# Joined exponentials, a transposed fold and a moved 1/sqrt in a two-layer Mamba, tree, attention and expert kernel

## The reference, cut to what matters

```python
# attention: 16 heads, 4 key/value heads, head width 64, causal, over each sequence
scores = einsum(q, k) / 8, masked above the diagonal
probs = softmax(scores)
out = (probs @ v) @ Wo
# experts: 64 experts, 8 for each token
scores = softmax(x @ gate_w.T)
topk_w, topk_ids = top_k(scores, 8);  topk_w /= topk_w.sum()
h = silu(x_e @ w_gate) * (x_e @ w_up);  out_e = h @ w_down
y = sum over the 8 of topk_w * out_e
# after each block
x = layernorm(x + block(x))
```

## Time and profile before

| | |
|---|---|
| time, median of 3 runs | 5111.49 us (5107.31 to 5113.56) |
| the profiled execution's own time | 5056.72 us |
| its span, first to last instruction | 5054.9 us |
| mean granted TensorE clock | 0.948 of full speed |
| attention, 1884 to 3712 us | 1828 us: TensorE busy 1767.73, VectorE 1575.48, ScalarE 1505.22, GpSimd 352.55 |
| route, 3712 to 4110 us | 398 us: TensorE 245.36, VectorE 182.49, ScalarE 116.57, GpSimd 277.73 |
| combine, 4892 to 5055 us | 163 us: VectorE 154.56, GpSimd 23.89, DMA engines 84% busy |

### The profile page before, as it was taken

The page is one execution under the profiler, slowest core; times in us unless marked ns, Lnnn a source line. Parts: engine busy times, 40 slices in busy tenths (PEclk is TensorE's granted clock), DMA queues, the critical chain, the costliest instruction groups (busy, mean ns, idle before and its releaser), DMA issues. The chain is left out here.

```text
span 5054.9 us, 84397 instructions
## 1 busy us (share of the span) xinstructions
PE 4342.6 (86%) x20410; PEld 3064.2 (61%) x20411; DVE 3700.1 (73%) x7521; ACT 2830.2 (56%) x6544; POOL 1747.8 (35%) x1517
## 2 busy tenths in 40 slices
PE   6887787769999879999999999999976649999960
PEld 2333333336666447888888888888865637777740
DVE  6999999966666678888888888888854433333349
ACT  6777777522222118888888888888843314444420
POOL 5777777620000011122121212122137743333321
PEclk8999999999999989999999999999987869999985
DMA  1000000021111461211121112212135445555558
GB/s 42 13 13 13 13 13 9 9 69 36 36 36 35 151 188 26 52 31 49 27 58 26 50 26 59 51 26 51 34 116 169 164 127 157 156 150 155 156 174 276
DMA packets 329081, 384.68 MB, mean 76 GB/s; under 512 B 124209, under 2 KB 263337, under 8 KB 323003
## 3 DMA queue, kind: packets, MB, share of 16 engines
q1 hardware_dynamic: 255931, 265.05, 17.8%
q0 software_dynamic: 26112, 73.44, 4.1%
q10 hardware_dynamic: 46944, 45.16, 3.3%
HBM read 230.26 MB, written 153.24 MB: 76 GB/s over the span
## 5 line engine op out<-in xcount | busy, mean ns | idle before, releaser
L1539 DVE TENSOR_TENSOR probsT<-ps_t,probsT 128x512 fp32r<-128x512 f32 (+3 forms) x1280 | 779.6, 609 | 137.8 <-ACT probsT L1479 116.2
L1479 ACT ACTIVATE probsT<-ps_t 128x512 fp32r<-128x512 f32 (+3 forms) x1280 | 686.6, 536 | 255.8 <-PE ps_t L1327 231.2
L1471 ACT ACTIVATE probs<-ps_s,negm 128x512 f32<-128x512 f32 (+3 forms) x1297 | 812.4, 627 | 28.1 <-DVE negm L1532 27.1
L1339 PE MATMUL ps_o<-probsT,vbuf 128*128 128x512 f32 (+3 forms) x2560 | 815.8, 402 | 6.8 <-ACT folding L1485 6.2
L1314 PE MATMUL ps_s<-kbuf,qbuf 128*128 (+1 forms) x2602 | 768.7, 380 | 59.2 <-ACT probs L1471 31.5
L1519 DVE TENSOR_REDUCE pmax<-ps_s 128x1 f32<-128x512 f32 (+3 forms) x1301 | 777.6, 600 | 48.6 <-PE ps_s L1314 24.3
L1327 PE MATMUL ps_t<-idn,probs 128*128 128x128 f32 x4352 | 694.8, 275 | 13.8 <-DVE probsT L1539 13.8
L445 POOL TENSOR_TENSOR dBx<-u,b_all 128x1024 f32<-128x1024 f32 x256 | 616.2, 2409 | 237.0 <-DVE h L531 226.3
L1327 PEld LDWEIGHTS ps_t<-idn,probs 128*128 128x128 f32 x4352 | 517.4, 142 | 135.2 <-DVE probsT L1539 41.0
L1314 PEld LDWEIGHTS ps_s<-kbuf,qbuf 128*128 128x128 f32 x2602 | 445.5, 189 | 179.0 <-issue 65.4
L1422 POOL CAST qbuf<-qstage 128x512 fp32r<-128x512 f32 x132 | 81.4, 616 | 1272.1 <-DMA qstage<-q_scr 748.1
(11 more groups left out here) (249 smaller groups left out, 7243.5 us busy)
## 6 DMA issues: line engine op xcount, KB each, us to landing
xr<-xs ACTq DMA_DIRECT2D x294, 136.0 KB
parts<-y SPq DMA_DIRECT2D x36, 1024.0 KB, 5.2
qstage<-q_scr SPq DMA_DIRECT2D x528, 64.0 KB
w_gu<-W_guT SPq DMA_DIRECT2D x64, 384.0 KB, 3.5
q_scr<-rot SPq DMA_DIRECT2D x64, 256.0 KB, 2.9
attn<-ostage SPq DMA_DIRECT2D x128, 128.0 KB, 2.0
at<-attn SPq DMA_DIRECT2D x32, 512.0 KB, 4.1
w_d<-W_downT SPq DMA_DIRECT2D x64, 192.0 KB, 3.7
```

The costliest lines, as they stand in the source:

```text
L1339: last = nc.tensor.matmul(ps_o[:, lo:], vbuf[:, kb, :, :], probsT[:, g % SLOTS, part, lo:], start=kb == 0 and part == 0, stop=kb == BAND * ...
L1471: nc.scalar.activation(probs[:, k, at:at + n, :], ps_s[:, u % RING, 0:n * P], ACT.Exp, bias=negm[:, tile, :], accum_out=sums[:, s, j, c:c ...
L1479: nc.scalar.activation(probsT[:, g % SLOTS, 0, lo:], ps_t[:, t % 2, lo:], ACT.Copy).then_inc(high_t.sem, 1)
L1539: nc.vector.tensor_tensor(probsT[:, g % SLOTS, 1, lo:], ps_t[:, t % 2, lo:], probsT[:, g % SLOTS, 0, lo:].bitcast(F32), ALU.subtract).then ...
```

## The change

Four parts.

1. **Joined exponentials.** A chunk that is not its tile's last and does not lie in the last bank of the ring is exponentiated together with the next one, in one ScalarE instruction over two PSUM banks (up to 1024 columns), at the first one's turn; the second one's turn has no `exps`. The semaphore rises by 2 at its end. `MERGE` pairs the chunks (0,1), (2,3), (5,6), (8,9), (10,11), (12,13) of unit 0 and (0,1), (3,4), (6,7), (10,11), (12,13), (16,17), (18,19) of unit 1: 13 pairs in a head. Since the exponentials run 16 chunks ahead, unit 0's chunks are done in unit 1's turns and the other way round.
2. **Fold by four transposes.** The fold is 4 transposes of 128x128 instead of 4 fp32 matmuls by `idn_2`. The two halves are no longer added by it: a new ScalarE copy `spill` takes the whole bank to `halves`, and GpSimd's `finish` adds the halves and multiplies by 1/sum. `normalise` leaves VectorE. The bank is released by `spill`. `spill` stands after `high` of turn `FOLD + 1`, before the next `exps`; the one of the short band right behind its `take`.
3. **Routing's 1/sqrt.** GpSimd's two instructions per tile go; ScalarE does Ln and Exp, and VectorE three small Newton instructions ahead of `norm`.
4. **Combining by whole rows.** Instead of two strided reductions VectorE adds 128x512 (`add_low`), 128x512 (`add_quarters`) and 128x256 (`add_last`), and GpSimd adds 128x512 and 128x256 (`add_high`) two tiles ahead. A `parts` slot is released after `add_quarters`.

```diff
@@ attention
+    MERGE = []
+    for k in range(NU):
+        ends, v = [None] * STEPS, 0
+        while v < STEPS:
+            s, j, c = CHUNKS[k][v]
+            two = c < s and (k * STEPS + v) % RING < RING - 1
+            ends[v] = 1 + two
+            v += 1 + two
+        MERGE.append(ends)
...
             def turn(hx, k, g):
                 s, kb = GROUPS[k][g]
                 t = use(k, g)
                 pe.wait_ge(exp_done.sem, exp_done.at(hx, band_end(k, s)))
-                pe.wait_ge(t_out.sem, t_out.at(hx, t - 1))
+                bank_free(hx, k, t)
...
                 for j in range(BAND):
-                    last = nc.tensor.matmul(ps_t[:, t % 2, j * HD:(j + 1) * HD], folding[:, j * P:(j + 1) * P], idn_2[:, :],
-                                            start=True, stop=True)
+                    last = nc.tensor.transpose(ps_t[:, t % 2, j * P:(j + 1) * P], folding[:, j * P:(j + 1) * P], idn[:, :])
...
+            def finish(hx, n):
+                s, half = QUEUE[n], halves[:, n % 2, :, :, :]
+                after(spilled.sem, spilled.at(hx, n + 1))
+                after(n_done.sem, n_done.at(hx, n))
+                nc.gpsimd.tensor_tensor(whole[:, :, :], half[:, :, 0, :], half[:, :, 1, :], ALU.add).then_inc(added.sem, 1)
+                after(added.sem, added.at(hx, n + 1))
+                after(r_done.sem, r_done.at(hx, n + 1))
+                after(o_out[s].sem, o_out[s].at(hx - 1))
+                nc.gpsimd.tensor_tensor(ostage[:, BAND * s:BAND * (s + 1), :], whole[:, :, :],
+                                        rinv[:, s, :, :].to_broadcast((P, BAND, HD)), ALU.mult).then_inc(n_done.sem, 1)
...
             def exps(hx, k, v):
+                if MERGE[k][v] is None:
+                    return
...
-                nc.scalar.activation(probs[:, k, at:at + n, :], ps_s[:, u % RING, 0:n * P], ACT.Exp, bias=negm[:, tile, :],
-                                     accum_out=sums[:, s, j, c:c + 1]).then_inc(exp_done.sem, 1)
+                nc.scalar.activation(probs[:, k, at:at + (hi - lo) // P, :].rearrange("p n t -> p (n t)"), ps_s[:, lo:hi], ACT.Exp,
+                                     bias=negm[:, tile, :], accum_out=sums[:, s, j, c:c + 1]).then_inc(exp_done.sem, MERGE[k][v])
...
+            def spill(hx, k, short):
+                n, t = 2 * k + short, fold_use(k, short)
+                act.wait_ge(f_done.sem, f_done.at(hx, n + 1))
+                act.wait_ge(added.sem, added.at(hx, n - 1))
+                nc.scalar.activation(halves[:, n % 2, :, :, :], ps_t[:, t % 2, :], ACT.Copy).then_inc(spilled.sem, 1)
...
                         high(hx, k, v)
                         if v == FOLD[k] - 1:
                             take(hx, k, 0)
+                        if v == FOLD[k] + 1:
+                            spill(hx, k, 0)
                     next_exps(STEPS)
                     take(hx, k, 1)
+                    spill(hx, k, 1)
@@ route
+            def inv_std(t):
+                h = t % 2
+                act.wait_ge(aggr.sem, aggr.at(t))
+                nc.scalar.activation(log[:, h, :], mv[:, h, 1:2], ACT.Ln, bias=eps_sb[:, :]).then_inc(log_done.sem, 1)
...
+                nc.scalar.activation(guess[:, h, :], log[:, h, :], ACT.Exp, scale=-0.5).then_inc(guessed.sem, 1)
...
+            nc.scalar.preload_act_table_set("natural_log_exp_and_others")
@@ route, gpsimd
             for t in range(NT):
-                if t + 3 < NT:
-                    inv_std(t + 3)
@@ combine
+            def add_high(t, s, loads):
+                h = s % 2
+                pool.wait_ge(in_ld[s].sem, 32 * loads)
+                pool.wait_ge(quarter.sem, quarter.at(t - 2))
+                nc.gpsimd.tensor_tensor(high[:, h, :, :], parts[:, s, HALF:HALF + 2, :], parts[:, s, HALF + 2:TOPK, :], ALU.add
+                                        ).then_inc(half_done.sem, 1)
+                pool.wait_ge(half_done.sem, half_done.at(t))
+                nc.gpsimd.tensor_tensor(high[:, h, 0, :], high[:, h, 0, :], parts[:, s, TOPK, :], ALU.add).then_inc(high_done.sem, 1)
...
+                    inv_std(SLOTS * i + s, s % 2)
+                    add_high(SLOTS * i + s + 2, (s + 2) % SLOTS, i + 1 + (s + 2) // SLOTS)
...
                     nc.vector.bn_stats(stats[:, h, :], r4[:, h, :]).then_inc(stat.sem, 1)
-                    total(*following, 0)
+                    add_low(t + 1, nxt, i + 1 + (s + 1) // SLOTS)
...
                     nc.vector.bn_aggr(mv[:, h, :], stats[:, h, :]).then_inc(aggr.sem, 1)
-                    total(*following, 1)
+                    add_quarters(t + 1, nxt)
+                    add_last(t + 1, nxt)
```

More of the change, by code:

```diff
@@ L1145, in fold_use, with before_use @@
         return k * TURNS + (TURNS - 1 if short else FOLD[k] + 1)
+    def before_use(k, t):
+        k, t = (k, t - k * TURNS - 2) if t - k * TURNS >= 2 else (k - 1, t - k * TURNS - 2 + TURNS)
+        if t == TURNS - 1 or t == FOLD[k] + 1:
+            return "fold", 2 * k + (t == TURNS - 1) + 1
+        return "turn", k * STEPS + t - (t > FOLD[k]) + 1
     def chunk(k, v, lead):
@@ L1150, in chunk, with span @@
         return n // PER, n % PER // STEPS, n % STEPS
+    MERGE = []
[7 more added lines that the diff above has]
+        MERGE.append(ends)
+    def span(k, v):
+        (s, j, c), more = CHUNKS[k][v], MERGE[k][v] - 1
+        bank = (k * STEPS + v) % RING
+        return bank * CW, (bank + more) * CW + blocks(s, j, c + more) * P
     sems = []
@@ L1317, in scores, with bank_free @@
                 if c == s:
-                    last = nc.tensor.matmul(ps_s[:, u % RING, w - P:w], idn_r[:, :], mask_r[:, :], start=False, stop=True)
+                    last = nc.tensor.matmul(ps_s[:, at + w - P:at + w], idn_r[:, :], mask_r[:, :], start=False, stop=True)
                 last.then_inc(s_done.sem, 1)
+            def bank_free(hx, k, t):
+                kind, count = before_use(k, t)
+                if kind == "fold":
+                    pe.wait_ge(spilled.sem, spilled.at(hx, count))
+                else:
+                    pe.wait_ge(low_t.sem, low_t.at(hx, count))
             def turn(hx, k, g):
@@ L1450, in _ @@
                 values(g + 1)
-                with pool.Fori(1, GROUP) as j4:
-                    head_queries(pool.snap(g * GROUP + j4))
-                for n, used in enumerate(V_USED):
-                    after(pv_done.sem, pv_done.at(g * GROUP + GROUP - 1, used))
-                    set_values(g + 1, n)
+                finish(g * GROUP, 0)
+                finish(g * GROUP, 1)
+                next_queries(g * GROUP, 1)
+                finish(g * GROUP, 2)
+                finish(g * GROUP, 3)
+                with pool.Fori(1, GROUP - 1) as j4:
+                    head(pool.snap(g * GROUP + j4))
+                end = pool.snap(g * GROUP + GROUP - 1)
+                next_queries(end, 0)
+                finish(end, 0)
+                finish(end, 1)
+                next_queries(end, 1)
+                for n in range(2):
+                    after(pv_done.sem, pv_done.at(end, V_USED[n]))
+                    set_values(g + 1, n)
+                finish(end, 2)
+                for n in range(2, BANDS):
+                    after(pv_done.sem, pv_done.at(end, V_USED[n]))
+                    set_values(g + 1, n)
+                finish(end, 3)
         @block.scalar
@@ L1518, in peak @@
                 dve.wait_ge(s_done.sem, s_done.at(hx, u + 1))
-                nc.vector.reduce_max(pmax[:, tile, c:c + 1], ps_s[:, u % RING, 0:blocks(s, j, c) * P],
+                at = u % RING * CW
+                nc.vector.reduce_max(pmax[:, tile, c:c + 1], ps_s[:, at:at + blocks(s, j, c) * P],
                                      axis=mybir.AxisListType.X).then_inc(cmax.sem, 1)
@@ L2411, in combine @@
         parts = sb("parts", [P, SLOTS, TOPK + 1, DM])
+        low = sb("low6", [P, 2, 2, DM])
+        high = sb("high6", [P, 2, 2, DM])
         r4 = sb("r4", [P, 2, DM])
```

155 lines of the change are left out of this document (93 added, 62 removed).

## The result

The changed kernel takes 5195.68 us (median of four, 5189.88 to 5209.47) against 5109.40 for the kernel before on the same chip: 1.0176 times as long, 95% interval 1.0160 to 1.0191, so +86 us. Forecast were 5142 us, +31, and a range up to 5190. The sign was right, the size was not.

A forecast was written before the change was run, and what follows sets the result against it. TensorE paces attention's full turns, a chain through ScalarE, VectorE and TensorE its band ends, GpSimd's scatters route. Attention +63, route -27 and combine -5 sum to +31 on the median: 5142 us, range 5050 to 5190.

The forecast's parts named there:

- 0.93 x 29 tiles: Route: scatters set the pace, so dropping GpSimd's two instructions saves 0.93 us a tile, -27 us; ends -28 and -15.
- I put the differences on the median.: Sum: +31 us added to the 5111.49 median gives 5142; from the profiled execution, 55 us faster, it would be 5088.
- Full pairs: Attention, full turns: a pair frees its first bank 0.43 us later; six places lose 0.24 us, 1.4 a head.
- The tail of unit 1: Attention, unit 1's turns 12 to 17: pairs and `spill` lengthen the chain by 0.43 + 0.18 + 0.39 + 0.43 = 1.43 us a head.
- The folds: Attention: four transposes save 0.45 us a fold, four times a head, partly lost; sum 0.85 us, bounds 0 and 1.8.
- a head of attention near 59.0 us rather than 57.0: Attention: sign that the forecast is right; heads under 57 us would show it wrong.
- 4.55 us a tile: Combine: VectorE's 1.8 and GpSimd's 2.7 us of adds run in a row on a shared port; -5 us in all.
- rival B: Combine's adds run side by side, 3.7 us a tile, -32 us there; total +4, 5115 us; chance 0.12.
- well over 1.28: Combine: sign that the forecast is right, GpSimd's 512-column adds taking longer than the 1.28 us of the profile.
- A: The forecast itself: pairs cost in attention, adds exclude each other; 5120 to 5185 us, chance 0.50.
- C: Attention gains: late banks fall into existing waits and folds count in full, -58 us; total -90, 5022 us; chance 0.15.
- D: Halves of A and C cancel in attention, leaving -27 - 5 = -32, 5080 us; chance 0.23.

The follow-up runs named there:

- 5061 job: One of three jobs, each on one chip, in which the unchanged kernel before took 5061 to 5065 us.
- 5110 job: One of two jobs, each on one chip, in which the unchanged kernel before took 5110 us, as in the main result.
- the second trace of before: Second profile of the kernel before, nothing changed: an execution of 5106.28 us with route at 445 us; its timed runs differed by -3 us.

## Why the prediction missed

**Route: the step that failed.** "Without GpSimd's two instructions a tile is 8 x 1.27 = 10.16, not 11.09 us: 0.93 x 29 tiles" was measured, to the microsecond, in a job of the profiled execution's kind: -28 us against -27. In one of the timed runs' kind it was +14. The step that failed stands in the sum: "I put the differences on the median." The profiled execution was 55 us faster than the median, and this was taken for an offset without a place. Nearly all of it lay in route, 398 against 445 us, because there the scatters did not set the pace. A price read from a closed list of GpSimd was put on runs whose list was not closed: in them GpSimd stood waiting for what TensorE's late signals led to. That accounts for 41 of the 55 us of the miss; attention adds 21 and combine takes 10 back.

**Attention: right in mechanism, three terms off the same way.** Forecast (1.4 + 1.43 - 0.85) x 32 = +63; measured +84, and 2.56 a head. Full pairs: six at 0.24 = 1.4 were forecast. The table has seven: 0.21 at three turns, 0.31 at unit 0's turn 14, which was left out for a wait that falls away in return, 0.13 + 0.10 at unit 1's turns 2 and 3 together, and 0.33 at two. Of these 1.83 some 0.28 come back at unit 0's turns 15 and 16 and unit 1's turn 1: 1.55. The tail of unit 1: 0.43 was forecast at turn 12 and 0.49 measured, 0.18 at turn 14 and 0.32, 0.39 + 0.43 at turn 16 and 0.81: 1.62 for 1.43. That turn 16 fits is luck: `spill` alone costs 0.65 there and the pairs alone 0.41, and the two do not add up. The folds: 0.85 was forecast, and beside the pairs they give 0.04 + 0.13 + 0.43 = 0.60; the one before unit 1 gives 0.37 when it is alone; the pair (16,17) before its `take`, which the prediction named, is the likely reason. Beyond the 0.28 the joined exponentials bring nothing in return: ScalarE is busy 1451 instead of 1505 us and waits 349 us for transposes. The sign "a head of attention near 59.0 us rather than 57.0" divides the stage by 32; by that measure it came to 59.8, while from copy to copy a head went from 56.36 to 58.92. That 59.0 seems to fit comes from mixing the two.

**Combine: right in mechanism, too dear.** Forecast 4.55 us a tile, measured 4.26, 13 to 15 us off rather than 5. The engines do exclude each other (rival B's 3.7 is refuted, as is its -32), but it hits other instructions than forecast. GpSimd's 512-column add was to be "well over 1.28" and took 1.26: it came first each time. VectorE paid, 0.93 at the scaling (median) and 0.25 at `add_low`, and so did GpSimd's 1/sqrt, 1.43 us for 0.74, which the prediction had kept at 0.75. On the other hand VectorE's stats ran beside GpSimd's second add at their usual 0.41; overlaps like this one are what 4.55 had left out. That it is these which make up the 0.29 is argued, not shown. The Trainium skill (SBUF — State Buffer, "Who interferes with whom") has scalings of this kind among the instructions that can take the shared port as well; the trace agrees with 1.25 against 0.41 us, and the prediction had applied the rule to adds only.

**The rivals.** A was the right one in attention in jobs of either kind; C (folds in full, pairs free) and D (attention as before) are refuted by +84. None of them had a route that gets slower, and the bound for it, -15, excluded one. In a 5061 job the whole change is +41, which the forecast's +31 and its own range would have held.

**What stays open.** In a 5110 job ScalarE and VectorE start up to 11.8 and 10.6 us after TensorE's work and they themselves were ready, because TensorE's signals come late, in the changed kernel mostly 3.7 us after the last scatter's start; in the others no `r` is late. What holds the signals, and what differs between the jobs, no run here shows. SyncE's load of a later tile's `at` is not enough to explain it: in the second trace of before an `r` that was 8.3 us late started 7 us after the load's last packet.

## What to carry to other kernels

When a profiled execution is 1% faster than the runs that it stands for, find the stage that the difference lies in before pricing anything in that stage, and price it for both kinds; a second profile, from another job, does it. Joining two instructions over a ring of buffers saves issue time on the engine that joins and holds the first buffer for the length of the second: where that engine is not the one waited for, it is a loss at every place whose slack is below that length. An engine that helps with half of the adds while it shares a path with the first one may be slower than none: here VectorE alone did 4.10 us a tile, with GpSimd's help 4.26.

## What the runs showed of the hardware that was not expected

- One program, two times by job: 5061 to 5065 and 5109 to 5110 us. Of the 50 us between two profiled executions 47 lie in one stage with 256 indirect DMAs by GpSimd (398 and 445 us).
- In the slower kind TensorE's semaphore signals in that stage come up to 14 us after the matmul's end in the profile, several together 0.06 us apart, and 12 to 14 of 32 `r` start late by it; in the faster kind all 32 come after 0.01 us. GpSimd's 16 scatters without a pause make it cost more (461 us) than 8 and a pause of 0.93 us (445).
- A VectorE scaling of 128x256 took 0.41 us alone and 1.25 to 1.34 when GpSimd had begun an add of 1.26 us; GpSimd's add of a single column took 0.19 us alone and 0.67 to 0.69 beside VectorE's add of 512 columns, its power of one column 0.55 and 0.74.
- An exponential of 1024 columns takes 1.117 us and its row sums end 1.20 us after its start; two of 512 take ScalarE 2 x 0.77 = 1.54 by the earlier trace rows.
